# Decoder layer on one core: ScalarE's order in the first two batches of the attention phase, and where batch 0's cosines are stored

## The chip, the cores and the metric

The kernel runs on one NeuronCore of a Trainium2 chip. The core has a matrix engine (TensorE, PE in the profile; PEld is its loading of stationary tiles), a vector engine (VectorE, DVE), an activation engine (ScalarE, ACT), a general engine (GpSimd, POOL) and a queue for synchronisation and DMA (SyncE, SP). Each works through its own instruction list in order, and they wait for each other through semaphores only. The metric is the device time of the program in microseconds (us), lower is better.

## The reference

A decoder layer on 16 batches of 128 x 1024 f32, in three blocks, each followed by an addition of its input and a layer norm:

```python
# 1: causal attention, 16 heads of 64, rotary q and k, w_q, w_k, w_v, w_out 1024 x 1024
scores = where(causal, einsum('bhqd,bhkd->bhqk', q, k), -1e9) / 8
out = einsum('bhqk,bhkd->bhqd', softmax(scores), v) @ w_out.T
# 2: a 3-tap convolution whose taps are weighted by cosines between neighbours of ctx
sim = stack([cos(e, left(e)), cos(e, e), cos(e, right(e))])     # per batch and position
out = einsum('bit,oi->bot', unfolded_x * repeat(sim, C), weight)
# 3: gated MLP with ternary weights: scale = mean|w|, round(w/scale) clipped to -1..1
out = bitlinear(silu(bitlinear(x, w_gate)) * bitlinear(x, w_up), w_down)    # 1024 -> 2752 -> 1024
```

The mean of |w| over each of the three MLP weights is needed before they can be rounded, so these weights are read twice.

## The kernel before

It is written by hand, engine by engine, with semaphores; nothing reorders it. Phase 1 has a prologue and 16 turns, one per batch b. In the prologue the four attention weights are loaded, batch 0's q, k and v are computed from the raw f32 weights (`first_qkv`), and each weight is scaled by its norm and split into a high and a low f16 part. ScalarE writes the high part of tile n (`high_w(n)`, L847), VectorE the low part (`split_w`, L1226); `high_w(n)` waits until the split of tile n-2 is done. Tiles 16 to 23 are w_v, 24 to 31 w_out, and the last of these splits happen in turn 0. The norms come from `square(n)` on ScalarE (L1005) and a small product on TensorE, `w_total(m)` (L573), which VectorE reads in `w_factors(m)`.

A turn b on TensorE: transposes of q and k (`qk_T`, L516), the six half products that make batch b+1's q, k and v (`proj(0..5)`, each 24 products of 128 x 512, L525), the scores of two groups of eight heads (`scores(0)`, `scores(1)`, L627), the transposes of the probabilities (`prob_T(0)`, `prob_T(1)`, L516), probabilities times v (`pv(0)`, `pv(1)`, L649), and the output product of the batch (`out_proj`). In turn 0 batch 1's halves 0 and 2 are already there, and batch 0's output product is computed in turn 1. A product half waits for its PSUM bank to be read: `proj(1)` for `v_chunk(0,1)` on ScalarE, `proj(3)` for the rotary step on VectorE (L1064, L1070). `proj(4)` in turn 0 also waits for the last split of w_v.

VectorE masks the scores and takes their maxima (`mask_max`, L1253 to L1258), ScalarE takes the exponentials with their sums (`exps`, L885, eight instructions per group of eight heads), VectorE normalises (L1266, L1267), TensorE transposes. Each transpose pair and each q/k pair fills two PSUM banks, which ScalarE copies out (`copy_bank`, L817), and `scores` and `pv` wait for these copies.

Beside this, ScalarE sums |w| of the MLP weights in turns 0 to 5: eight chunks of 128 x 1376 a turn (`abs_chunk`, L862), through two buffers (`wch`). SP loads a chunk (`w_load`, L400) when the one that lay in its buffer has been summed. `abs_chunk(-5)` in turn 1 is chunk 3 of turn 0. SP's list holds, in this order, the loads of the chunks, of the transposed x of batch b+2 (L418), of ctx (L423, and L424 for a shifted row), of the residual (L434), and the stores of the three cosine rows (L476, waits for POOL's cosines) and of the block's result (L393). The order on each engine is the order of calls in the function `turn` of that engine; for batches 0 and 1 it is written out apart (`turn_first`, and `if second`), batches 2 to 5 and 6 to 13 are loops.

Phase 2 (convolution and MLP, one turn per batch) follows after turn 15 and begins when phase 1's products are done.

Of the kernel before, what the change touches and what calls it, by code (L numbers as in the profile page):

```python
# [79 lines left out]
def decoder(nc, x, xT_in, ctx, wqT, wkT, wvT, woT, w_ffn, conv_w, cos, sin, causal, ident, out):  # L80
# [4 lines left out]
    with ExitStack() as stack:  # L85
# [270 lines left out]
        def _(sp):  # L356
# [37 lines left out]

            def turn(b, mode, has_next, has_next2):
# [29 lines left out]
                if second:  # L425
                    w_load(0)
                    w_load(1)
                    store_x1(0, xres)
# [31 lines left out]
                if mode != "plain":  # L460
                    for c in range(2, SUMS if mode == "sum" else CUTS):
                        if mode == "cut":
                            w_store(c - 2)
                        w_load(c)
                    if mode == "cut":
                        w_store(CUTS - 2)
                        w_store(CUTS - 1)
# [4 lines left out]
                sp.wait_ge(sims_ready, b + 1)  # L472
                for j, row in ((0, 1), (1, 2), (1, 0)):
                    off = 1 if row == 0 else 0
                    dst = sim_dram[bass.ds(b, 1), row, off:off + D].rearrange("o (p t) -> p (o t)", t=8)
                    sp.dma_start(dst, cosines[:, j]).then_inc(sims_stored, 16)  # L476
# [33 lines left out]
        def _(pe):  # L510
# [99 lines left out]
            def turn(b, mode, has_next, has_next2):  # L610
# [68 lines left out]
                if isinstance(b, int) and b == 0:  # L679
                    qk_T(0)  # L680
                    proj(1)
                    scores(0)
                    qk_T(1)
                    proj(3)
                    scores(1)
                    prob_T(0)
                    proj(4)
                    pv(0)
                    proj(5, 0)
                    prob_T(1)  # L690
                    proj(5, 1)
                    pv(1)
                    pe.wait_ge(roped, 6)
                    transposes(tr_pair(1, 0), [s[:, t * P:(t + 1) * P] for s in (q, k) for t in range(4)])
                    return
# [50 lines left out]
            w_total(3)  # L746
# [66 lines left out]
        def _(act):  # L813
# [42 lines left out]
            def turn(b, mode, has_next, has_next2):  # L856
# [45 lines left out]
                def turn_first():  # L902
                    for w in range(2):
                        copy_bank(w, tr_pair(0, 0), qkT[:, w])
                    for n in range(2 * KT + 4, 3 * KT + 1):
                        high_w(n)
                    act.wait_ge(scores_full, 1)
                    for w in range(2):
                        copy_bank(w, tr_pair(0, 1), qkT[:, w])
                    abs_chunk(0)  # L910
                    exps(0)
                    high_w(3 * KT + 1)
                    for w in range(2):
                        copy_bank(w, tr_pair(0, 2), probT[:, w])
                    exps(1)
                    high_w(3 * KT + 2)
                    oT_high_part(0)
                    abs_chunk(1)
                    act.wait_ge(pv_full, 1)
# [3 lines left out]
                    high_w(3 * KT + 3)  # L923
                    v_chunk(1, 0)
                    v_chunk(1, 1)
                    oT_high_part(1)
                    high_w(3 * KT + 4)
# [7 lines left out]

                if first:
                    turn_first()
                    return
                second = isinstance(b, int) and b == 1
                if not second:  # L940
                    for w in range(2):
                        copy_bank(w, tr_pair(b, 0), qkT[:, w])
# [3 lines left out]
                if second:  # L946
                    abs_chunk(-5)
                exps(0)
                if second:
                    abs_chunk(-4)  # L950
                    abs_chunk(-3)
                elif has_next:
                    ctx_square()
                if not second:
                    abs_chunk(0)
# [5 lines left out]
                if second:  # L961
                    abs_chunk(-2)
                    abs_chunk(-1)
                    ctx_square()
                    abs_chunk(0)
# [54 lines left out]
            square(3 * KT + 7)  # L1020
# [727 lines left out]
```

## Time and profile before

| | |
|---|---|
| time, median of 3 runs | 1411.73 us (1410.52 to 1412.89) |
| the profiled execution | 1411.03 us, of which the span from first to last instruction is 1409.2 us |
| PE busy | 1365.5 us (97%) |
| DVE busy | 1063.0 us (75%) |
| ACT busy | 623.2 us (44%) |
| POOL busy | 214.1 us (15%) |
| mean granted TensorE clock | 0.992 of full |

A row of the timeline gives the start and the duration of a run of like instructions in us, the engine, the source line, output and input tiles, the shapes, the count, and in brackets the idle time of the engine before it and what ended it. f32 products show two records each. Turn 0 begins on TensorE after w_v's products at 62.8 us, turn 1 with a product at 104.80, turn 2 at 172.96.

### The profile page before, as it was taken

The page shows a single profiled execution, that of the slowest core. Times are in us where ns is not written, and L with a number is a line of the kernel's source. Part 1 is how long each engine was busy: PE and PEld are TensorE (multiplying, and loading weights), DVE is VectorE, ACT ScalarE, POOL GpSimd, SP SyncE. Part 2 cuts the span into 40 slices and gives each one's busy share as a digit, 9 for nine tenths or more (in the row PEclk, how much of TensorE's full clock was granted, in tenths as well). Part 3 has the DMA queues.
Part 4 walks back from the last instruction along what each step waited for, and adds up shares of the span by engine and source line. Part 5 has one row for each costly group of instructions (what it writes and reads, how often), then busy time and mean ns, then how long its engine had stood idle before and what let it go on. Part 6 is the DMA issues. An engine that isn't in the chain of part 4 may idle for free.

```text
span 1409.2 us, 23219 instructions
## 1 busy us (share of the span) xinstructions
PE 1365.5 (97%) x7562; PEld 691.9 (49%) x7562; DVE 1063.0 (75%) x1859; ACT 623.2 (44%) x1208; POOL 214.1 (15%) x257
## 2 busy tenths in 40 slices
PE   8989899999999999999999999999999999999997
PEld 3445455555545545554554554444444444444443
DVE  6978355456488677777868778888888888888884
ACT  6867454474455455545535452232222223222321
POOL 0002212213131221221322212000000000000000
PEclk9989999999999999999999999999999999999999
DMA  9514454454434435454453584222222222222200
GB/s 379 220 41 149 154 199 146 138 184 148 169 113 158 162 113 174 141 164 141 140 185 107 133 276 133 76 74 74 74 74 74 74 74 74 74 74 74 74 20 25
DMA packets 63878, 178.96 MB, mean 127 GB/s; under 512 B 15408, under 2 KB 26848, under 8 KB 63840
## 3 DMA queue, kind: packets, MB, share of 16 engines
q1 hardware_dynamic: 63840, 178.48, 38.8%
q8 instruction: 20, 0.33, 0.1%
q14 instruction: 18, 0.15, 0.0%
HBM read 153.02 MB, written 25.43 MB: 127 GB/s over the span
## 4 chain that ended last, share of the span: by engine, by line
issue 42%; PE 42%; POOL 4%; DVE 4%; DMA 4%; ACT 2%; SPq 1%; POOLq 0%; ACTq 0%; DVEq 0%
PE ps L525 32%; PE ps L516 3%; DMA ctx<-ctx 3%; PE ps L595 3%; PE ps L649 2%; PE ps L627 2%; POOL q L1635 1%; DVE weights L1226 1%; ACT prob L885 1%; POOL simw L1688 1%; POOL rstd L1630 1%; ACT weights L847 1%; POOL k L1617 1%; DMA wch<-w_ffn 0%; DMA x_scratch<-weights 0%
## 5 line engine op out<-in xcount | busy, mean ns | idle before, releaser
L525 PE MATMUL ps<-weights,xT 128*128 128x512 f16 x2112 | 473.5, 381 | 0.9 <-ACT v L833 0.9
L525 PEld LDWEIGHTS ps<-weights,xT 128*128 128x128 f16 x2112 | 204.8, 98 | 238.0 <-issue 8.9
L759 PE MATMUL ps<-weights 128*128 128x512 fp8e4 (+1 forms) x1536 | 300.0, 357 | 0.9 <-DMA weights<-ternary_scratch 0.9
L759 PEld LDWEIGHTS ps<-weights 128*128 128x128 bf16 x1536 | 146.9, 98 | 155.8 <-issue 1.3
L525 PE MATMUL ps<-weights 128*128 128x512 f16 x768 | 168.9, 379 | 1.5 <-DVE weights L1272 1.5
L780 PE MATMUL ps<-weights 128*128 128x512 fp8e4 x704 | 158.4, 381 | 0.0
L1030 ACT ACTIVATE weights<-ps,xscale 128x512 f32<-128x512 f32 x96 | 61.8, 644 | 171.7 <-PE ps L759 171.7
L885 ACT ACTIVATE prob<-prob,negmax,undo 128x128 f32<-128x128 f32 x256 | 122.8, 484 | 9.1 <-DVE negmax L1258 9.1
L525 PEld LDWEIGHTS ps<-weights 128*128 128x128 f16 x768 | 75.1, 98 | 90.9 <-DVE weights L1272 1.7
L780 PEld LDWEIGHTS ps<-weights 128*128 128x128 bf16 x704 | 68.0, 98 | 76.8 <-issue 1.8
L1630 POOL TENSOR_TENSOR rstd<-rstd,expo 128x1 f32<-128x1 f32 x32 | 17.9, 559 | 523.8 <-DVE rstd L1152 491.0
L817 ACT COPY qkT<-ps 128x512 f32<-128x512 f32 x64 | 34.3, 588 | 139.3 <-PE ps L516 139.3
L854 ACT CAST weights<-weights 128x1024 f16<-128x1024 f32 x48 | 50.2, 1047 | 69.0 <-DVE weights L1179 64.0
L862 ACT ACTIVATE wch<-wch 128x1376 f32<-128x1376 f32 x48 | 64.6, 1346 | 27.5 <-DMA wch<-w_ffn 27.5
L837 ACT ACTIVATE xT<-weights,magic,xscale 128x1024 f32<-128x1024 f32 x16 | 19.9, 1242 | 127.6 <-DVE xscale L1203 127.6
L1543 DVE SCALAR_TENSOR_TENSOR weights<-ps,xscale,weights 128x512 f32<-128x512 f32 x96 | 65.9, 687 | 7.2 <-PE ps L759 6.8
L1244 DVE SCALAR_TENSOR_TENSOR tern<-wch,thr,below 128x1376 fp8e4<-128x1376 f32 x24 | 55.4, 2308 | 17.8 <-ACT below L877 14.6
L1617 POOL TENSOR_TENSOR k<-rope_c,rope_s 128x512 f32<-128x512 f32 x28 | 41.0, 1463 | 183.1 <-issue 95.5
L1064 DVE SCALAR_TENSOR_TENSOR rope_c<-ps,cosb 128x512 f32<-128x512 f32 x58 | 39.8, 686 | 34.6 <-PE ps L525 29.5
L555 PE MATMUL ps<-weights 128*128 128x512 f16 x288 | 64.8, 379 | 0.0
L1617 POOL TENSOR_TENSOR q<-rope_c,rope_s 128x512 f32<-128x512 f32 x28 | 36.7, 1311 | 162.9 <-DVE rope_s L1070 162.8
L1536 DVE TENSOR_REDUCE hmax<-weights 128x1 f32<-128x512 f32 x96 | 59.9, 624 | 1.2
(171 smaller groups left out, 1813.0 us busy)
## 6 DMA issues: line engine op xcount, KB each, us to landing
wch<-w_ffn SPq DMA_DIRECT2D x96, 688.0 KB, 4.3
wch<-sim_scratch SPq DMA_DIRECT2D x96, 128.0 KB
ternary_scratch<-tern SPq DMA_DIRECT2D x48, 172.0 KB, 1.9
ctx<-ctx SPq DMA_DIRECT2D x16, 512.0 KB
wo_raw<-x_scratch SPq DMA_DIRECT2D x16, 512.0 KB, 3.3
x_in<-xT_in SPq DMA_DIRECT2D x15, 512.0 KB, 6.7
weights<-x SPq DMA_DIRECT2D x15, 512.0 KB, 10.4
x_scratch<-weights SPq DMA_DIRECT2D x15, 512.0 KB, 2.9
```

The lines of the kernel that those rows point to most:

```text
L525: ins = nc.tensor.matmul(ps[:, bank], partsT[:, a, t], weights[:, t, w, half * HALF:(half + 1) * HALF], start=(t == 0 and a + w == 0), sto ...
L555: ins = nc.tensor.matmul(ps[:, c], convw_parts[:, w, kk], conv_parts[:, kk, a, c * HALF:(c + 1) * HALF], start=(kk == 0 and a + w == 0), s ...
L759: ins = nc.tensor.matmul(ps[:, 2 * w + a, 0:n], xqT[:, t], w8m[:, t, at:at + n], start=(t == 0), stop=(t == KT - 1))
L780: return nc.tensor.matmul(ps[:, AC + c], hT[:, t], down8[:, t, c * HALF:(c + 1) * HALF], start=(t == 0), stop=(t == IT - 1))
L854: nc.scalar.copy(conv_parts[:, kk, 0], convG[:, kk + 1]).then_inc(conv_high, 1)
L862: nc.scalar.activation(wch[:, c % 2], wch[:, c % 2], ACT.Abs, accum_out=abs_part[:, bass.ds(b * SUMS + c, 1)]).then_inc(wch_free[c % 2], 1)
L885: ins = nc.scalar.activation(prob[:, r, t], prob[:, r, t], ACT.Exp, scale=undo[:, 0, 0:1], bias=negmax[:, r, t:t + 1], accum_out=rowsum[:, ...
L1030: nc.scalar.activation(silu[:, w, 0:n], ps[:, 2 * w, 0:n], ACT.Silu, scale=xscale[:, 1:2]) \
L1244: nc.vector.scalar_tensor_tensor(out=tern[:, c % 2], in0=wch[:, c % 2], scalar=thr[:, 0:1], in1=below[c % 2], op0=ALU.is_gt, op1=ALU.min, ...
L1536: return st.done(nc.vector.tensor_reduce(hmax[:, c:c + 1], hbuf[:, at:at + n], AX_X, ALU.max, apply_absolute_value=True))
L1543: nc.vector.scalar_tensor_tensor(out=hbuf[:, at:at + n], in0=ps[:, 2 * w + 1, 0:n], scalar=xscale[:, 2:3], in1=silu[:, w, 0:n], op0=ALU.mu ...
L1617: nc.gpsimd.tensor_tensor((q, k)[j % 2][:, j // 2 * HALF:(j // 2 + 1) * HALF], rope_c[:], rope_s[:], ALU.add) \
```

## The change

On ScalarE: (a) the square of tile 31 moves from before batch 0's v copies to behind turn 0's first q/k copies. (b) In turn 0, `high_w(24)` moves from before the second q/k copies to behind the first exponentials, the sum of chunk 0 from before these exponentials to behind `high_w(24)`, `high_w(25)` from before the first probability copies to behind them, `high_w(26)` to behind the first output part and the sum of chunk 1, and `high_w(27)` to behind the v copies and the second output part. (c) Turn 1 has a function of its own, `turn_second`: sum -2 stays ahead of the second exponentials and sum -1 behind them, ahead of the ctx square; the last probability copies stand ahead of sums 2 and 3; sums 4 and 5 stand behind the first v copy instead of ahead of the output part. On TensorE (d) `w_total(3)` moves from the end of the prologue into the middle of `proj(1)`. On SP (e) batch 0's cosines are stored in turn 1, behind chunk loads 0 and 1 (turn 0 ends without them), and chunk loads 2 and 3 of turn 1 stand ahead of the store of batch 0's result.

ScalarE in turn 0, from w_out's last square on, before. `tern,wsq<-wo_raw` is the square of tile 31, `weights<-weights,wnorm` a high part, `qkT` and `probT` the copies out of PSUM, `prob,rowsum` the exponentials, `wch,abs_part` a sum of |w|:

```order
L1005 ACTIVATE tern,wsq<-wo_raw 128x1024
L829 ACTIVATE v<-ps,scale 128x512 x2
L817 COPY qkT<-ps 128x512 x2
L847 ACTIVATE weights<-weights,wnorm 128x1024 x5
L817 COPY qkT<-ps 128x512 x2
L862 ACTIVATE wch,abs_part<-wch 128x1376
L885 ACTIVATE prob,rowsum<-prob,negmax,undo 128x128 x8
L847 ACTIVATE weights<-weights,wnorm 128x1024
L817 COPY probT<-ps 128x512 x2
L885 ACTIVATE prob,rowsum<-prob,negmax,undo 128x128 x8
```

The same place now:

```order
L838 ACTIVATE v<-ps,scale 128x512 x2
L826 COPY qkT<-ps 128x512 x2
L1038 ACTIVATE tern,wsq<-wo_raw 128x1024
L856 ACTIVATE weights<-weights,wnorm 128x1024 x4
L826 COPY qkT<-ps 128x512 x2
L894 ACTIVATE prob,rowsum<-prob,negmax,undo 128x128 x8
L856 ACTIVATE weights<-weights,wnorm 128x1024
L871 ACTIVATE wch,abs_part<-wch 128x1376
L826 COPY probT<-ps 128x512 x2
L856 ACTIVATE weights<-weights,wnorm 128x1024
L894 ACTIVATE prob,rowsum<-prob,negmax,undo 128x128 x8
```

The first exponentials now follow the second q/k copies directly; a high part and a sum stood between.

ScalarE in turn 1, from the first probability copies on, before (`sq<-ctx` is the ctx square, `weights<-ps` a high part of the attention output):

```order
L817 COPY probT<-ps 128x512 x2
L885 ACTIVATE prob,rowsum<-prob,negmax,undo 128x128 x8
L862 ACTIVATE wch,abs_part<-wch 128x1376 x2
L900 ACTIVATE sq<-ctx 128x1152
L862 ACTIVATE wch,abs_part<-wch 128x1376 x2
L893 CAST weights<-ps 128x512
L862 ACTIVATE wch,abs_part<-wch 128x1376 x2
L817 COPY probT<-ps 128x512 x2
L862 ACTIVATE wch,abs_part<-wch 128x1376 x2
```

And now:

```order
L826 COPY probT<-ps 128x512 x2
L871 ACTIVATE wch,abs_part<-wch 128x1376
L894 ACTIVATE prob,rowsum<-prob,negmax,undo 128x128 x8
L871 ACTIVATE wch,abs_part<-wch 128x1376
L909 ACTIVATE sq<-ctx 128x1152
L871 ACTIVATE wch,abs_part<-wch 128x1376
L902 CAST weights<-ps 128x512
L871 ACTIVATE wch,abs_part<-wch 128x1376
L826 COPY probT<-ps 128x512 x2
L871 ACTIVATE wch,abs_part<-wch 128x1376 x2
```

Three sums stand between the second exponentials and the second probability copies where six stood: one of the six is now ahead of the exponentials, two are behind the copies.

SP from turn 0's last six chunk loads to turn 1's result store, before:

```order
L400 DMA wch<-w_ffn 128x1376 x6
L476 DMA sim_scratch<-cosines 128x8 x3
L418 DMA x_in<-xT_in 128x1024
L423 DMA ctx<-ctx 128x1024
L424 DMA ctx<-ctx 127x128
L400 DMA wch<-w_ffn 128x1376 x2
L393 DMA x_scratch<-weights 128x1024
```

And now:

```order
L408 DMA wch<-w_ffn 128x1376 x6
L426 DMA x_in<-xT_in 128x1024
L431 DMA ctx<-ctx 128x1024
L432 DMA ctx<-ctx 127x128
L408 DMA wch<-w_ffn 128x1376 x2
L401 DMA sim_scratch<-cosines 128x8 x3
L408 DMA wch<-w_ffn 128x1376 x2
L393 DMA x_scratch<-weights 128x1024
```

The x and ctx loads no longer stand behind the store of the cosines.

```diff
@@ SP @@
                 if second:
                     w_load(0)
                     w_load(1)
+                    store_sims(0)
+                    w_load(2)
+                    w_load(3)
                     store_x1(0, xres)
...
-                    for c in range(2, SUMS if mode == "sum" else CUTS):
+                    for c in range(4 if second else 2, SUMS if mode == "sum" else CUTS):
...
-                sp.wait_ge(sims_ready, b + 1)
-                for j, row in ((0, 1), (1, 2), (1, 0)):
...
+                if not (isinstance(b, int) and b == 0):
+                    store_sims(b)
@@ TensorE, turn 0 @@
                     qk_T(0)
-                    proj(1)
+                    proj(1, 0)
+                    w_total(3)
+                    proj(1, 1)
                     scores(0)
...
             for m in range(3):
                 first_qkv(m)
-            w_total(3)
@@ ScalarE, turn_first @@
                     for w in range(2):
                         copy_bank(w, tr_pair(0, 0), qkT[:, w])
-                    for n in range(2 * KT + 4, 3 * KT + 1):
+                    square(4 * KT - 1)
+                    for n in range(2 * KT + 4, 3 * KT):
                         high_w(n)
                     act.wait_ge(scores_full, 1)
                     for w in range(2):
                         copy_bank(w, tr_pair(0, 1), qkT[:, w])
+                    exps(0)
+                    high_w(3 * KT)
                     abs_chunk(0)
-                    exps(0)
-                    high_w(3 * KT + 1)
                     for w in range(2):
                         copy_bank(w, tr_pair(0, 2), probT[:, w])
+                    high_w(3 * KT + 1)
                     exps(1)
-                    high_w(3 * KT + 2)
                     oT_high_part(0)
                     abs_chunk(1)
+                    high_w(3 * KT + 2)
...
@@ ScalarE, turn 1 @@
+                def turn_second():
+                    act.wait_ge(scores_full, 3)
+                    for w in range(2):
+                        copy_bank(w, tr_pair(1, 1), qkT[:, w])
+                    abs_chunk(-5)
+                    exps(0)
+                    abs_chunk(-4)
+                    abs_chunk(-3)
+                    act.wait_ge(pv_full, 2)
+                    for w in range(2):
+                        copy_bank(w, tr_pair(1, 2), probT[:, w])
+                    abs_chunk(-2)
+                    exps(1)
+                    abs_chunk(-1)
+                    ctx_square()
+                    abs_chunk(0)
+                    oT_high_part(0)
+                    abs_chunk(1)
+                    act.wait_ge(pv_full, 3)
+                    for w in range(2):
+                        copy_bank(w, tr_pair(1, 3), probT[:, w])
+                    abs_chunk(2)
+                    abs_chunk(3)
+                    oT_high_part(1)
+                    v_chunk(2, 0)
+                    abs_chunk(4)
+                    abs_chunk(5)
+                    v_chunk(2, 1)
+                    high_x(3)
+                    abs_chunk(6)
+                    abs_chunk(7)
@@ ScalarE, prologue @@
             high_w(2 * KT + 3)
-            square(3 * KT + 7)
             v_chunk(0, 0)
```

## Rows read from the trace of the kernel before

**Rows 1.** Part 2 of the page: busy tenths of PE in 40 slices of the span.
```profile
PE   8989899999999999999999999999999999999997
```
**Rows 2.** Timeline of PE, turn 0 and the first product of turn 1.
```profile
64.38 0.39 PE L573 MATMUL ps<-wsq,tern 128*128 128x8 f32 x2 [1.57 <-ACT tern L1005]
...
70.90 1.16 PE L627 MATMUL ps<-qkT 64*128 64x128 f32 x16
...
72.94 5.34 PE L525 MATMUL ps<-weights,xT 128*128 128x512 f16 x24
80.20 1.84 PE L627 MATMUL ps<-qkT 64*128 64x128 f32 x16 [1.92 <-ACT qkT L817]
86.24 1.97 PE L516 MATMUL ps<-idf,prob 128*128 128x128 f32 x8 [4.20 <-DVE prob L1267]
88.01 6.70 PE L525 MATMUL ps<-weights,xT 128*128 128x512 f16 x24
...
104.80 5.34 PE L525 MATMUL ps<-weights,xT 128*128 128x512 f16 x24 [0.86 <-ACT v L833]
```
**Rows 3.** Timeline of PE, turn 1 to the start of turn 3.
```profile
123.64 1.09 PE L516 MATMUL ps<-idf,prob 128*128 128x128 f32 x8
...
153.98 1.98 PE L649 MATMUL ps<-probT,v 128*64 128x128 f32 x16 [6.53 <-ACT probT L817]
155.89 6.87 PE L525 MATMUL ps<-weights,xT 128*128 128x512 f16 x24
...
172.96 0.60 PE L516 MATMUL ps<-idf,q 128*128 128x128 f32 x4
...
223.29 0.60 PE L516 MATMUL ps<-idf,q 128*128 128x128 f32 x4
```
**Rows 4.** Stretches: us, busy (x instructions) of PE, PEld, DVE, ACT, POOL; clock; DMA.
```profile
76.60:114.03 37.43, 30.45 (x185) 17.28 (x184) 27.30 (x51) 28.21 (x59) 0.00 (x0) 0.86 0.12 39
80.50:90.70 10.20, 6.00 (x31) 4.00 (x28) 5.21 (x10) 7.53 (x24) 0.00 (x0) 0.50 0.22 71
152.10:159.00 6.90, 5.02 (x24) 2.79 (x25) 0.00 (x0) 3.52 (x7) 0.38 (x1) 0.51 0.79 236
```
**Rows 5.** Timeline of ACT, turn 0, around the second q/k copies.
```profile
77.99 1.15 ACT L847 ACTIVATE weights<-weights,wnorm 128x1024 f16<-128x1024 f32 x1 [5.20 <-DVE weights L1226]
...
79.99 1.36 ACT L862 ACTIVATE wch<-wch 128x1376 f32<-128x1376 f32 x1
...
81.33 0.49 ACT L885 ACTIVATE prob<-prob,negmax,undo 128x128 f32<-128x128 f32 x1
```
**Rows 6.** Timeline of DVE, turn 0 and the start of turn 1.
```profile
72.05 0.75 DVE L1070 SCALAR_TENSOR_TENSOR rope_s<-ps,sinb 128x256 f32<-128x256 f32 x2
...
76.46 0.23 DVE L1258 TENSOR_SCALAR negmax<-negmax,undo 128x4 f32<-128x4 f32 x1
...
85.28 0.18 DVE L1266 RECIPROCAL rinv<-rowsum 128x4 f32<-128x4 f32 x1 [1.00 <-ACT prob L885]
...
86.11 1.28 DVE L1226 SCALAR_TENSOR_TENSOR weights<-weights,wnorm 128x1024 f16<-128x1024 f32 x1
...
114.03 0.69 DVE L1064 SCALAR_TENSOR_TENSOR rope_c<-ps,cosb 128x512 f32<-128x512 f32 x1
...
121.18 2.21 DVE L1267 TENSOR_TENSOR prob<-prob,rinv 128x512 f32<-128x512 f32 x1
```
**Rows 7.** Timeline of ACT, turn 1, up to the second probability copies.
```profile
140.20 1.16 ACT L900 ACTIVATE sq<-ctx 128x1152 f32<-128x1152 f32 x1 [4.79 <-DMA ctx<-ctx]
...
149.78 1.35 ACT L862 ACTIVATE wch<-wch 128x1376 f32<-128x1376 f32 x1 [4.40 <-DMA wch<-w_ffn]
...
152.83 1.05 ACT L817 COPY probT<-ps 128x512 f32<-128x512 f32 x2
```
**Rows 8.** Timeline of SP's queue, the end of turn 0's list and the ctx load.
```profile
129.44 1.29 SPq L476 DMA_DIRECT2D sim_scratch<-cosines  x3
...
131.30 0.38 SPq L423 DMA_DIRECT2D ctx<-ctx  x1
```

More of the change, by code:

```diff
@@ L393, in store_x1, with store_sims @@
                 sp.dma_start(x1_dram[bass.ds(n, 1)].rearrange("o s d -> s (o d)"), src).then_inc(x1_stored, 16)
+            def store_sims(n):
+                sp.wait_ge(sims_ready, n + 1)
+                for j, row in ((0, 1), (1, 2), (1, 0)):
+                    off = 1 if row == 0 else 0
+                    dst = sim_dram[bass.ds(n, 1), row, off:off + D].rearrange("o (p t) -> p (o t)", t=8)
+                    sp.dma_start(dst, cosines[:, j]).then_inc(sims_stored, 16)
             def turn(b, mode, has_next, has_next2):
@@ L471, in turn @@
                     store_x1(b - 1, xres)
-                sp.wait_ge(sims_ready, b + 1)
-                for j, row in ((0, 1), (1, 2), (1, 0)):
-                    off = 1 if row == 0 else 0
-                    dst = sim_dram[bass.ds(b, 1), row, off:off + D].rearrange("o (p t) -> p (o t)", t=8)
-                    sp.dma_start(dst, cosines[:, j]).then_inc(sims_stored, 16)
+                if not (isinstance(b, int) and b == 0):
+                    store_sims(b)
                 if not has_next:
@@ L922, in turn_first @@
                     high_x(2)
-                    high_w(3 * KT + 3)
                     v_chunk(1, 0)
@@ L926, in turn_first @@
                     oT_high_part(1)
+                    high_w(3 * KT + 3)
                     high_w(3 * KT + 4)
@@ L938, in turn @@
                     return
[L939 to L942, printed above, removed]
+                if isinstance(b, int) and b == 1:
+                    turn_second()
+                    return
+                for w in range(2):
+                    copy_bank(w, tr_pair(b, 0), qkT[:, w])
                 act.wait_ge(scores_full, b * 2 + 1)
@@ L945, in turn @@
                     copy_bank(w, tr_pair(b, 1), qkT[:, w])
-                if second:
-                    abs_chunk(-5)
                 exps(0)
[L949 to L952, printed above, removed]
+                if has_next:
                     ctx_square()
-                if not second:
-                    abs_chunk(0)
+                abs_chunk(0)
                 sign_chunk(0)
@@ L960, in turn @@
                 exps(1)
[L961 to L965, printed above, removed]
                 abs_chunk(1)
```

## The prediction

> **What bounds the kernel now.** I read the busy slices first: TensorE is at nine tenths or more from the sixth slice of 35 us almost to the end [rows 1]. Turn 2 takes 223.29 - 172.96 = 50.33 us [rows 3], and that is TensorE's own work, so from 172.96 us on an edit elsewhere can gain nothing, and an engine that is late by less than its slack costs nothing. What is to be had lies before 172.96. Second I read TensorE's timeline there, for the brackets: idle 1.57 us before `w_total(3)`, 1.92 before the second scores, 4.20 before the first probability transposes, 0.86 before turn 1's first product [rows 2], and 6.53 before `pv(1)` of turn 1 [rows 3]. That is 15.08 us. Third I read the granted clock: it is 0.50 in 80.5 to 90.7 and 0.51 in 152.1 to 159.0 [rows 4]. The first stretch begins right behind the 1.92 us gap, the second inside the 6.53 us one. TensorE was busy for 6.00 and 5.02 us in them; at full rate it would have needed half, so the low clock costs 3.0 and 2.5 us. The rows agree: the product at 88.01 lasts 6.70 and not 5.34 us, the scores at 80.20 1.84 and not 1.16 [rows 2]. In all about 20.5 us can be won at the most.
>
> **The change, part by part.**
>
> *The square and `w_total(3)`.* They leave the 1.57 us gap, but the gap isn't won. `proj(3)` needs the PSUM bank that VectorE's rotary step reads until 72.05 + 0.75 = 72.8 [rows 6], and VectorE's list up to there is unchanged; it starts at 72.94 now [rows 2] and would start at about 72.9 again. TensorE waits some 1.1 us at that point instead of 1.57 earlier. Value: 0. In its new place `w_total(3)` needs a square that now runs behind four copies, an estimated 2 us later than the 64.38 of before [rows 2], and TensorE gets there after half a product, at about 67.0; if this cover of 0.6 fails, VectorE's factors come late by the same, and it has no slack. I take 0, with 0 to 0.5 as the bounds.
>
> *The second q/k copies.* ScalarE holds them back behind a high part that waits until 77.99 for VectorE [rows 5]. Their input, the transposes behind the scores of 70.90, is done by 72.9 at the latest, so they now run at about 72.7 and the scores start when `proj(3)` ends, 72.94 + 5.34 = 78.3, less the overlap of 0.1 with the next. Value: the 1.92 us of idle.
>
> *The exponentials.* They start at 81.33 now, behind a sum that began at 79.99 [rows 5]. Both maxima are there at 76.46 + 0.23 = 76.7 [rows 6], the first 1.6 earlier, at 75.1. So they run from 75.15; the second four, due at 77.1, don't wait. From their start to VectorE's last reciprocal it is 85.28 - 81.33 = 3.95 us [rows 5, 6], which gives 79.1. From there to the transposes it is 86.24 - 85.28 = 0.96, so they start at 80.1, 6.1 us earlier. The scores end at 79.4, and 0.7 us of idle stay.
>
> *The v product behind them.* It needs the last w_v split as well, which VectorE runs after normalising: 86.11 - 85.28 + 1.28 = 2.1 us behind the reciprocal [rows 6], at 81.2. So it starts at 81.3 where it was 88.01 [rows 2]: 6.7 us earlier, and at full clock it lasts 5.34 and not 6.70, so it ends 8.1 us earlier.
>
> *The rest of turn 0.* TensorE's next pieces have 8.1 us of lead and VectorE must give as much. From 76.60 to 114.03 VectorE is busy for 27.30 of 37.43 us [rows 4]; 10.1 us are idle. The exponentials' waits go, and so does the wait for a transpose that ran at half clock. What stays is the 0.14 or so per small semaphore wait, some 0.8 us for ScalarE's high part of x, and 0.3 in w_out's splits: about 2.0. VectorE reaches turn 1 at 114.03 - 8.1 = 105.9. The sums of chunks 0 and 1, and w_out's high parts, fill holes of ScalarE, which is busy for 28.21 of the 37.43. Turn 1's first product starts at about 96.4 (0.75 of the 0.86 idle is found again, as a wait for the low part of x). From that product to turn 1's probability transposes TensorE has 123.64 - 104.80 = 18.8 us of work [rows 2, 3]: 115.2. VectorE gets from its turn start to the second normalised half in 121.18 + 2.21 - 114.03 = 9.4 us [rows 6]: 115.3. The two meet, so VectorE is the next bound there, and any microsecond that it loses TensorE loses. Value of turn 0: 123.64 - 115.35 = 8.3 us (bounds 6.5 and 9).
>
> *Turn 1.* `pv(1)` waits for copies that start at 152.83, behind sums whose chunks come late (4.40 us before the one of 149.78) and behind the ctx square, which waited 4.79 for its load until 140.20 [rows 7]. The ctx load was issued at 131.30, behind the cosine store, which held SP until 129.44 [rows 8]. Now SP gets to it after chunk load 7. That load goes out when sum -3 is done, at about 123.6 before and 115.3 now, so ctx is issued at 116.2 and, with the same 140.20 - 131.30 = 8.9 us, is there at 125.1. ScalarE behind it: exponentials 120.5 to 124.5, sum -1 to 125.9, ctx square to 127.0, sum 0, whose chunk is issued at 119.7 and lands after 7.7 us at the slowest that a chunk took in this stretch, to 128.9, the output part to 129.4, sum 1 to 131.5 (its chunk issued at 126.0, with 4 us; at 7.7 us: 135.2). The transposes to be copied end at about 134.0, so the copies are done at 135.0, with the slow load at 136.2. TensorE comes to `pv(1)` at 155.89 - 1.98 - 6.53 - 8.3 = 139.1. The cover is 4 us, or 3. All of the wait goes: 6.53 us, and with it the clock loss of 2.5. Value: 9.0 us (bounds 4 and 9.2).
>
> *The tail of turn 1.* ScalarE must give batch 3's high x, and VectorE the low one, before turn 2's first product at 172.96 + 0.87 - 17.3 = 156.5. Sums 4 and 5 now stand ahead of it. Their chunks are issued behind the store and reload of the residual, at about 138, and land at 142 and 144; the sums end at 145.5, high x at 147.2 and the low part at 148.5. 8 us of cover: 0. The cosine store in its new place waits for POOL's cosines, which come 8.3 us earlier too, at 121.1, before SP gets there at 126: 0. Turn 2 finds the same list at the same distances, 0.
>
> *Sum.* 8.3 + 9.0 = 17.3 us, taken down to 17.1 because two engines meet at the end of turn 0. 1411.03 - 17.1 = 1393.9 us for the execution profiled (its span would be 1392.1). The median of the runs is 0.7 above this execution, so between them 1394.2.
>
> **The clock, by row and by rule.** In the rows the clock fell behind a gap of 1.92 us and not behind one of 1.57 or 0.86 [rows 2, 4]. What I leave in turn 0 is 1.1, then 0.7 and 0.3 with a transpose between them, all below 1.57, so the clock should hold.
>
> The Trainium skill ("TensorE: Matmul & The Clock Gate", Part 1) says that half rate is the default, that activity releases it, and that the gate runs freely beside the program, so that one kernel meets it in another phase each run. By that rule two gaps of 0.7 and 0.3 near the 1.1 could still fall badly in some executions; the traces show one execution each and can't exclude it. It is the first rival below.
>
> **Rivals.**
>
> *The clock falls once all the same in turn 0.* For: 2.1 us of idle stay between 71.8 and 81.3. Against: they are in three pieces. The price is the 3.0 us of that stretch [rows 4], of which VectorE's own path hides a little: 14.5 us gained, 1396.5.
>
> *VectorE bounds turn 0 and takes back some of it.* It meets TensorE at 115.3. If its waits for ScalarE (high x, w_out's high parts, one of which now stands behind the copies of `prob_T(1)`) stay at 4 us rather than 2, all is late by 2: 15.3 gained, 1395.7.
>
> *Turn 1's wait shrinks but stays.* For: chunk loads share the engines of the DMA with ctx, x and each other, and one took 7.7 us. If sums 0 and 1 each find their chunk 3 us later than I say, the copies end at 141 or 142 and TensorE waits 2 to 3; with a gap like that the clock falls too, 2.5 us: 12 gained, 1399.
>
> *Slower.* The cosine store stands in front of turn 1's chunk loads 2 and 3. SP can't pass it, and behind it stand the residual's store, its reload and the loads of chunks 4 and 5, whose sums are ahead of high x of batch 3. If POOL's cosines came late, turn 2's first product would be late. It decides from 126 us on, the time at which SP gets there, first eats 8 us of cover, and then costs one for one; to lose more than the 17.1 the cosines would have to come after 126 + 8 + 17 = 151, 30 us after the 121.1 worked out above. At 155 it would give 1415. Against it: POOL is empty there.
>
> *Nothing happens*, because the gaps were set by something else: the brackets name ScalarE's instructions for 1.92 and 6.53, and the 4.20 stands behind a late exponential. 1411.
>
> **Chances.** Forecast (16 to 18.5 us gained) 0.68; the clock falls once 0.11; VectorE takes some back 0.09; turn 1's wait stays in part 0.08; slower 0.02; nothing 0.02. The likeliest gives 1394.2, with 1392.5 to 1396 as its own range. Below, the bounds of the parts add up to 18.2, and the bound of all is 20.5, so I go to 1391.8; above, I take in the clock and VectorE and half of the case with turn 1's wait: 1398.8. All of these but the last two are faster. About 0.2% (2.8 us) can be told from no change here. Faster 0.96, same 0.02, slower 0.02.
>
> **What would show it.** In the profile after: no bracket over 1.3 us on TensorE before turn 2; the second scores at 78.2, the first probability transposes at 80.1, the v product at 81.3 and 5.34 long; turn 1's first product near 96.4 and its first probability transposes near 115.3, VectorE's last normalising just ahead of them; `pv(1)` of turn 1 at 139 with no idle; turn 2 at 155.7; the clock at 1.00 from 60 us on; the ctx square of batch 1 near 126. It is wrong if a gap stands before `pv(1)`, if a half-clock stretch remains, or if turn 2's own length is no longer 50.33.

## The result and the profile after

The changed kernel takes 1393.95 us (median of 4 runs, 1391.7 to 1394.55) against 1411.36 us for the kernel before (4 runs, 1410.52 to 1412.89): ratio 0.9869, 95% interval 0.9857 to 0.9880 (the medians by themselves give 0.9877). It is 17.4 us faster; forecast were 17.1 us and 1394.2. The profiled execution took 1394.44 us with a span of 1392.6.

TensorE's timeline, turn 0 and the first product of turn 1 (columns as in [rows 2]):

```profile
64.76 2.75 PE L533 MATMUL ps<-weights,xT 128*128 128x512 f16 x12 [0.91 <-ACT v L838]
...
73.11 5.34 PE L533 MATMUL ps<-weights,xT 128*128 128x512 f16 x24 [0.76 <-DVE rope_s L1102]
78.38 1.16 PE L635 MATMUL ps<-qkT 64*128 64x128 f32 x16
80.23 1.09 PE L524 MATMUL ps<-idf,prob 128*128 128x128 f32 x8 [0.69 <-DVE prob L1299]
81.47 5.34 PE L533 MATMUL ps<-weights,xT 128*128 128x512 f16 x24
...
96.62 5.35 PE L533 MATMUL ps<-weights,xT 128*128 128x512 f16 x24 [0.57 <-DVE xT L1152]
```

The brackets of 1.92 and 4.20 us [rows 2] are gone and 0.69 is left; the 1.57 before `w_total(3)` has become 0.91 and 0.76. The product behind the probability transposes is 5.34 us long again, not 6.70. Turn 1's first product starts at 96.62 where it was 104.80.

The same in turn 1, up to the start of turn 3:

```profile
115.54 1.09 PE L524 MATMUL ps<-idf,prob 128*128 128x128 f32 x8
...
139.28 1.10 PE L657 MATMUL ps<-probT,v 128*64 128x128 f32 x16
140.31 5.35 PE L533 MATMUL ps<-weights,xT 128*128 128x512 f16 x24
...
155.86 0.60 PE L524 MATMUL ps<-idf,q 128*128 128x128 f32 x4
...
206.14 0.60 PE L524 MATMUL ps<-idf,q 128*128 128x128 f32 x4
```

The product after `pv(1)`, 6.87 us long before [rows 3], takes 5.35. `pv(1)` has no bracket where 6.53 us stood [rows 3]. Turn 2 starts at 155.86 instead of 172.96, 17.10 us earlier, and is 50.28 us long as before. ScalarE, turn 1, the rows that answer to [rows 7]:

```profile
126.71 1.17 ACT L909 ACTIVATE sq<-ctx 128x1152 f32<-128x1152 f32 x1 [0.54 <-DMA ctx<-ctx]
...
133.83 1.07 ACT L826 COPY probT<-ps 128x512 f32<-128x512 f32 x2 [2.02 <-PE ps L524]
```

The ctx square no longer waits 4.79 us, and ScalarE now waits for TensorE before the probability copies, not the other way round. What ends last at turn 1's first probability transposes is VectorE's normalising, which is done at 115.48 where the transposes start at 115.54:

```profile
113.27 2.21 DVE L1299 TENSOR_TENSOR prob<-prob,rinv 128x512 f32<-128x512 f32 x1
```

Two stretches of the kernel after: all of turns 0 and 1, and one much later (columns as in [rows 4]):

```profile
60.00:155.86 95.86, 92.78 (x537) 47.81 (x537) 75.36 (x132) 72.58 (x144) 17.61 (x21) 1.00 0.38 126
821.50:824.90 3.40, 2.92 (x7) 1.03 (x8) 2.02 (x6) 1.30 (x2) 0.00 (x0) 0.50 1.04 385
```

Both half-clock stretches of [rows 4] are gone, but a new one of 3.4 us stands in turn 15, in code that the change doesn't touch. (One more, in the last 20 us, is in both traces, behind a gap of 3.78 us that both have.) The rows at that place, of the kernel before:

```profile
834.66 1.09 PE L516 MATMUL ps<-idf,prob 128*128 128x128 f32 x8 [0.54 <-DVE prob L1267]
836.68 1.09 PE L649 MATMUL ps<-probT,v 128*64 128x128 f32 x16 [0.93 <-DVE weights L1272]
839.25 5.35 PE L525 MATMUL ps<-weights 128*128 128x512 f16 x24 [1.47 <-DVE weights L1272]
```

and of the kernel after:

```profile
817.39 1.09 PE L524 MATMUL ps<-idf,prob 128*128 128x128 f32 x8 [0.54 <-DVE prob L1299]
819.42 1.09 PE L657 MATMUL ps<-probT,v 128*64 128x128 f32 x16 [0.93 <-DVE weights L1304]
821.98 6.79 PE L533 MATMUL ps<-weights 128*128 128x512 f16 x24 [1.47 <-DVE weights L1304]
```

The gaps are the same to the hundredth; in one execution the clock holds and in the other it falls and costs 6.79 - 5.35 = 1.44 us. That is why the spans differ by 16.6 and not 17.1 us (0.9 us were won elsewhere in the rest). Differences of 1 to 2 us between single executions can be of this kind. So the experiments below are read by their medians and, where that is finer, by the time from `proj(3)` of turn 0 to turn 2 on TensorE: 100.02 us before, 82.75 after.

### The profile page after: what moved, and what is told of

Read it like the earlier page. It is cut to its first block, busy times and chain, and to the rows that moved or that the text cites. A ratio compares the mean times of both kernels' runs of the same rounds, so it can differ in the third digit from the quotient of the medians.

```text
span 1392.6 us, 23220 instructions
## 1 busy us (share of the span) xinstructions
PE 1362.0 (98%) x7562; PEld 689.2 (49%) x7562; DVE 1063.5 (76%) x1859; ACT 622.4 (45%) x1208; POOL 215.7 (15%) x257
## 4 chain that ended last, share of the span: by engine, by line
PE 51%; issue 40%; POOL 3%; DVE 2%; DMA 2%; ACT 1%; SPq 0%; POOLq 0%; ACTq 0%; DVEq 0%
PE ps L533 40%; PE ps L524 4%; PE ps L603 3%; PE ps L657 2%; PE ps L635 2%; DMA ctx<-ctx 1%; POOL q L1667 1%; POOL rstd L1662 1%; ACT prob L894 1%; DVE weights L1258 1%; POOL simw L1720 0%; PE ps L563 0%; ACT weights L856 0%; DMA weights<-wqT 0%; POOL k L1649 0%
## 5 line engine op out<-in xcount | busy, mean ns | idle before, releaser
L826 ACT COPY qkT<-ps 128x512 f32<-128x512 f32 x64 | 34.3, 588 | 133.8 <-PE ps L524 133.8
```

## The experiments

Each ran beside the kernel before (medians of it 1412.08, 1412.53 and 1412.89 us in the three groups), 4 runs each unless said. Differences "over the changed kernel" are against 1393.95, which was measured beside a median of 1411.36. The kernel before drifts by 1.5 us between these groups, so a difference of less than that is not settled by medians, and the TensorE time decides.

**Turn 0 alone.** The kernel before with the change's lines of turn 0:

```diff
-            w_total(3)            # end of TensorE's prologue
+                    proj(1, 0); w_total(3); proj(1, 1)
-  turn_first of the kernel before
+  turn_first of the change, square(31) in it
```

> The kernel before with turn 0's part of the change alone (square, w_total(3), ScalarE's order in turn 0). My theory: the two gaps of 1.92 and 4.20 us and the first half-clock stretch go, and turn 1 keeps its 6.53 us wait before pv(1) and the low clock behind it. Turn 1's first product at 96.6 us, turn 2 at 172.96 - 8.2 = 164.8, time 8.2 us under the kernel before. Rival (the order in turn 0 only matters together with the earlier loads, as turn 1's chunks and ctx come when they come): turn 1's wait grows by what turn 0 wins, and the time moves by less than 3 us.

Measured: 1404.57 us (1403.27 to 1406.19), 7.5 under the kernel before, ratio 0.9946 (0.9930 to 0.9963). From `proj(3)` to turn 2 it takes 91.84 us, 8.2 less than before. TensorE at `pv(1)` of turn 1:

```profile
146.29 1.98 PE L649 MATMUL ps<-probT,v 128*64 128x128 f32 x16 [6.55 <-ACT probT L818]
```

The wait of 6.53 stands there unchanged as 6.55, with the half clock behind it. What turn 0 wins is kept whole, and the rival, a longer wait in turn 1, is out.

**Turn 1 alone.** The change with turn 0 put back:

```diff
-  turn_first of the change; proj(1, 0); w_total(3); proj(1, 1)
+  turn_first of the kernel before; proj(1), w_total(3) in the prologue
```

> The change with turn 0 (ScalarE, w_total(3)) put back as in the kernel before; turn 1's ScalarE order and SP's list are the new ones. My theory: the parts add up, so this wins what turn 0 alone does not: no wait before pv(1) of turn 1, no half clock there, the gaps of 1.92 and 4.20 us and the half clock in turn 0 remain; 8.9 us under the kernel before. Rival (the parts overlap): under 5 us.

Measured: 1403.60 us (1402.49 to 1405.81), 8.5 under the kernel before, ratio 0.9938 (0.9922 to 0.9955). `pv(1)` has no gap. From `proj(3)` to turn 2: 90.99, 9.0 less. 8.2 + 9.0 = 17.2 of 17.27: the two parts add up.

**The square and `w_total(3)` put back.**

```diff
+            square(3 * KT + 7)     # again ahead of v_chunk(0, 0)
-                    square(4 * KT - 1)
-                    proj(1, 0); w_total(3); proj(1, 1)
+                    proj(1)        # w_total(3) again in the prologue
```

> The changed kernel with the last square and w_total(3) back where they were (the square ahead of batch 0's v copies, w_total(3) at the end of the prologue). The prediction gave this part 0: a gap of 1.4 to 1.6 us before w_total(3), none before the first half product, and proj(3) starting where it does now, for VectorE. Time within 0.3 us of the changed kernel, unless the gap brings the clock down (1.7 us for a short stretch). Rival: the 1.57 us were real and come back, 0.7 to 1.5 us.

Measured: 1393.98 us (1392.81 to 1394.9), ratio 0.9864 (0.9846 to 0.9881), that is 0.0 over the changed kernel. The gap is back, and `proj(3)` starts within 0.2 us of the 73.11 of the changed kernel; from there to turn 2 it is 82.77 against 82.75:

```profile
64.72 0.39 PE L581 MATMUL ps<-wsq,tern 128*128 128x8 f32 x2 [1.54 <-ACT tern L1036]
...
73.28 5.34 PE L533 MATMUL ps<-weights,xT 128*128 128x512 f16 x24
```

A gap of 1.5 us on the busiest engine is worth nothing here, since VectorE's rotary step sets the start of `proj(3)`.

**One high part ahead of the second q/k copies.**

```diff
-                    for n in range(2 * KT + 4, 3 * KT):
+                    for n in range(2 * KT + 4, 3 * KT + 1):
...
                     exps(0)
-                    high_w(3 * KT)
                     abs_chunk(0)
```

> The change with one high part (tile 24) back ahead of turn 0's second q/k copies; the exponentials still stand ahead of the sum. Theory A (the high part, which waits for a split on VectorE until 78 us, is what costs in turn 0): the second scores start at 80.2, the exponentials at about 80.1, the probability transposes at 85.0 after a gap of 3.7 us, the clock falls, and the time is 4.8 us of idle and 2 to 3 us of low clock over the changed kernel: 7.5. Theory B (the sum ahead of the exponentials costs as much as the high part): 2 us of idle over the changed kernel, 2 to 4 in all.

Measured: 1400.81 us (1399.97 to 1401.58), 6.9 over the changed kernel, ratio 0.9920 (0.9902 to 0.9938); `proj(3)` to turn 2 is 6.5 us longer. ScalarE, and TensorE behind it:

```profile
78.53 1.15 ACT L856 ACTIVATE weights<-weights,wnorm 128x1024 f16<-128x1024 f32 x1 [5.20 <-DVE weights L1257]
79.59 1.05 ACT L826 COPY qkT<-ps 128x512 f32<-128x512 f32 x2
```
```profile
80.74 1.16 PE L635 MATMUL ps<-qkT 64*128 64x128 f32 x16 [1.92 <-ACT qkT L826]
85.45 1.97 PE L524 MATMUL ps<-idf,prob 128*128 128x128 f32 x8 [3.55 <-DVE prob L1298]
```

One instruction of 1.1 us that waits 5.20 for VectorE brings back 1.92 + 3.55 - 0.69 = 4.8 us of idle and the half clock, as theory A said. From `proj(3)` to the probability transposes it is 13.30 us before [rows 2], 11.97 here and 7.12 in the changed kernel: 4.85 us hang on the high part, and the other 1.33, the length of a sum, on the sum that stood behind it in the kernel before.

**The sum ahead of the first exponentials.**

```diff
+                    abs_chunk(0)
                     exps(0)
                     high_w(3 * KT)
-                    abs_chunk(0)
```

> The change with the sum of chunk 0 back ahead of turn 0's first exponentials, behind the early q/k copies. Theory A: ScalarE is idle there for 1.39 us anyway, waiting for VectorE's maxima, so the sum of 1.33 us fills the hole and the exponentials start at 75.3 as now: 0, within 0.3 us of the changed kernel. Theory B: the exponentials come 1.3 us later and everything behind them too: 1.3 us over the changed kernel, and a gap of 2 us before the probability transposes with the low clock that follows one.

Measured: 1394.83 us (1394.15 to 1395.25), ratio 0.9875 (0.9857 to 0.9893), 0.9 over the changed kernel by the medians, where 0.3 at the most was expected; but `proj(3)` to turn 2 is 82.76 against 82.75, so nothing of it is from the edit's place. ScalarE:

```profile
73.97 1.36 ACT L871 ACTIVATE wch<-wch 128x1376 f32<-128x1376 f32 x1
...
75.48 0.49 ACT L894 ACTIVATE prob<-prob,negmax,undo 128x128 f32<-128x128 f32 x1
```

The sum fits in the hole before the maxima. Of the change's edits in turn 0 the place of the sum is worth nothing once the copies are early. Behind late copies it was worth the 1.33 us of the run above.

**SP's list as before, ScalarE's order new.**

```diff
-                    store_sims(0)
-                    w_load(2)
-                    w_load(3)
                     store_x1(0, xres)
...
-                    for c in range(4 if second else 2, SUMS if mode == "sum" else CUTS):
+                    for c in range(2, SUMS if mode == "sum" else CUTS):
...
-                if not (isinstance(b, int) and b == 0):
-                    store_sims(b)
+                store_sims(b)
```

> The change with SP's list as before (cosines stored at the end of turn 0, ahead of the x and ctx loads; chunk loads 2 and 3 of turn 1 behind the result's store). The theory of the prediction: the cosine store holds the ctx load back, so the ctx square and with it the probability copies come later; SP gets to it at 121.3, ctx is issued at about 123 instead of 116.6 and lands about 132, the square ends at 133, sums 0 and 1 at about 137 to 139, the copies at 140: 1 to 2 us of wait before pv(1), and the time 1 to 2 us (or 4, with the clock) over the changed kernel. Rival: the order on ScalarE is all of it, the copies are in time even so, and the time is that of the changed kernel within 0.5 us.

Measured: 1397.04 us (1395.32 to 1398.74), 3.1 over the changed kernel, ratio 0.9889 (0.9873 to 0.9906). ScalarE and TensorE in turn 1:

```profile
132.82 1.17 ACT L905 ACTIVATE sq<-ctx 128x1152 f32<-128x1152 f32 x1 [6.17 <-DMA ctx<-ctx]
...
137.60 1.06 ACT L822 COPY probT<-ps 128x512 f32<-128x512 f32 x2
```
```profile
148.35 10.52 PE L529 MATMUL ps<-weights 128*128 128x512 f16 x48 [2.22 <-DVE weights L1300]
```

The ctx square comes 6.1 us later, as I had it (132.8, 133 expected), but the copies are done at 138.7, in time for `pv(1)`, which has no gap. The time is lost one step later: the output product waits 2.22 us for the second part of the attention output, which ScalarE holds behind sums 2 and 3. `proj(3)` to turn 2 is 85.15 us, 2.4 longer. Expected were 1 to 2 us with the clock at full, as it is here, so the size was somewhat too small and the place wrong.

**The cosine store alone put back.**

```diff
-                    store_sims(0)
                     w_load(2)
                     w_load(3)
...
-                if not (isinstance(b, int) and b == 0):
-                    store_sims(b)
+                store_sims(b)
```

> The changed kernel with batch 0's cosine store back at the end of turn 0's list, ahead of the x and ctx loads; chunk loads 2 and 3 of turn 1 stay ahead of the result's store. In the run with SP's whole list as before, the copies for pv(1) were in time (137.6), and TensorE waited 2.2 us before the output product, for the second part of the attention output, which ScalarE had behind sums 2 and 3. Theory L (the loads behind the store and its reload were the cause): 0 to 0.3 us over the changed kernel, no gap before the output product, the ctx square at about 132.5. Theory C (the cosine store was): a gap of 1.5 us or more, 2 to 3 us over the changed kernel.

Measured: 1399.44 us (1398.88 to 1400.47), 5.5 over the changed kernel, ratio 0.9907 (0.9890 to 0.9925). TensorE:

```profile
147.27 5.34 PE L531 MATMUL ps<-weights 128*128 128x512 f16 x24 [1.06 <-DVE weights L1302]
154.67 7.04 PE L531 MATMUL ps<-weights 128*128 128x512 f16 x24 [2.06 <-ACT v L840]
```

and SP's queue:

```profile
122.07 1.29 SPq L401 DMA_DIRECT2D sim_scratch<-cosines  x3
...
123.94 0.38 SPq L431 DMA_DIRECT2D ctx<-ctx  x1
...
124.69 13.52 SPq L408 DMA_DIRECT2D wch<-w_ffn  x4
138.25 0.44 SPq L393 DMA_DIRECT2D x_scratch<-weights  x1
145.73 0.33 SPq L444 DMA_DIRECT2D weights<-x  x1
```

Theory L, that the place of the loads was the cause, is wrong. Theory C names the right edit, the cosine store, but not the way or the size: it said one gap of 1.5 us or more and 2 to 3 us in all. With the cosine store early, ctx late and chunk loads 2 and 3 ahead of the result's store, that store slips to 138.25 (132.22 in the changed kernel) and its reload to 145.73, chunks 4 and 5 with it. Since the change sums 4 and 5 stand ahead of the second v copy, so the second half of the output product waits 2.06 us for its bank, the clock falls behind it, and all is 5.2 us longer from `proj(3)` to turn 2.

**Chunk loads 2 and 3 alone put back.**

```diff
                     store_sims(0)
-                    w_load(2)
-                    w_load(3)
                     store_x1(0, xres)
...
-                    for c in range(4 if second else 2, SUMS if mode == "sum" else CUTS):
+                    for c in range(2, SUMS if mode == "sum" else CUTS):
```

> The changed kernel with chunk loads 2 and 3 of turn 1 back behind the store of batch 0's result and its reload; the cosine store stays in turn 1. Theory L: their chunks land at about 142 and 144 instead of 134.3 and 138.7, sums 2 and 3 end at about 145, the second output part comes at 146 and TensorE waits 1 to 2 us before the output product: 1 to 3 us over the changed kernel. Theory C: no gap, 0. A third outcome, no gap in either, means that each half alone has enough cover and only both together cost.

Measured: 1394.35 us (1391.59 to 1395.79), ratio 0.9862 (0.9844 to 0.9881), `proj(3)` to turn 2 82.76: nothing. With this the four combinations of SP's two edits are complete, all with the new order on ScalarE:

| time, and `proj(3)` to turn 2, us | loads 2 and 3 ahead of the result's store | behind it |
|---|---|---|
| cosine store in turn 1 | 1393.95, 82.75 | 1394.35, 82.76 |
| cosine store in turn 0 | 1399.44, 87.90 | 1397.04, 85.15 |

Moving the cosine store wins 2.7 us (2.4 on TensorE) with the loads behind and 5.5 (5.2) with them ahead. Moving the loads wins nothing beside the moved store and loses 2.4 (2.8) without it.

**SP's new list alone, ScalarE's order old.**

```diff
+                    store_sims(0)
+                    w_load(2)
+                    w_load(3)
                     store_x1(0, xres)
...                                       # and the rest of the change's diff under SP
```

> The kernel before with SP's new list alone. Theory of the prediction: the ctx load comes 5 us earlier or more, the six sums still stand before the probability copies, so the wait before pv(1) shrinks from 6.53 to about 1 us, below what the clock falls behind; but then sums, output part and high x come in the old order and chunks 2 and 3 early: 5 to 8 us under the kernel before. Rival (the number of sums ahead of the copies sets the wait, not SP's list): under 2 us.

Measured (10 runs): 1410.35 us (1407.17 to 1414.69), 1.7 under the kernel before, ratio 0.9990 (0.9977 to 1.0004): not told from no change. TensorE:

```profile
150.94 1.98 PE L657 MATMUL ps<-probT,v 128*64 128x128 f32 x16 [2.45 <-ACT probT L825]
...
160.66 10.52 PE L533 MATMUL ps<-weights 128*128 128x512 f16 x48 [1.94 <-DVE weights L1280]
```

The wait at `pv(1)` shrinks from 6.53 to 2.45 and 1.94 of it turn up before the output product. `proj(3)` to turn 2 is 2.3 us shorter; from turn 1's first product on it is 3.0, and turn 0, which the edit doesn't touch, came out 0.7 longer in this execution. Expected were 5 to 8; the rival's "under 2" is nearer. Neither ScalarE's order nor SP's list does in turn 1 what both do. SP's list is worth about as much on TensorE under the old order of ScalarE, 2.3 to 3.0 us here, as under the new, 2.4 in the run with SP's list as before.

**Four reductions more on VectorE at the end of turn 0.**

```diff
                     split_w(3, range(4, KT))
+                    for i in range(4):      # hmax is not used in phase 1
+                        nc.vector.tensor_reduce(hmax[:, i:i+1], rope_c[:], AX_X, ALU.max)
```

> The changed kernel with four reductions of 0.6 us (128 x 512) more on VectorE behind w_out's last split, at the end of turn 0; their results are not used. The prediction says that VectorE is the next bound there and has no slack against TensorE at turn 1's first probability transposes: all of the 2.4 us come out, a gap of 2.4 before those transposes, and 2.4 us over the changed kernel, 4 with a short stretch of half clock behind the gap. Rival (VectorE has slack there): less than 1.2 us.

Measured: 1397.53 us (1396.73 to 1399.27), 3.6 over the changed kernel, ratio 0.9890 (0.9872 to 0.9907):

```profile
117.92 1.24 PE L524 MATMUL ps<-idf,prob 128*128 128x128 f32 x8 [2.36 <-DVE prob L1299]
```

2.4 us more on VectorE are 2.36 us of wait on TensorE, and 1.7 of low clock behind it: VectorE has no slack there, as forecast. On TensorE it is 4.1 us from `proj(3)` to turn 2, by the medians 3.6; 4 were expected with a stretch of low clock.

**A gap of 2 us and one of 3 before `proj(3)`.** Two and four reductions ahead of the rotary step:

```diff
                     split_w(2, range(4, 6))
+                    # 2 (or 4) times: tensor_reduce(unused, mask of 128 x 512, min)
                     rope(1, 1)
```

> The changed kernel with two reductions of 0.6 us (128 x 512) more on VectorE ahead of the rotary step that proj(3) waits for in turn 0; their results are not used. The gap before proj(3) grows from 0.76 to 2.0 us. Theory A (a gap of 1.9 us brings the clock down, one of 1.57 does not): all is 1.2 us later, and a stretch of half clock begins behind the gap and costs 2 to 3 us: 3 to 4 in all. Theory B (the clock falls only by the sum of idle around it, and the 1.92 us gap of before fell together with the 4.20 one behind it): 1.2 us, and the clock stays at 1.00.

> As the one with two reductions, with four: the gap before proj(3) grows to 3.2 us and all is 2.4 us later. Both theories of the clock expect it to fall here: 2.4 us of delay and 1.7 to 3 us of low clock, 4 to 5.5 in all over the changed kernel. If the clock stays at 1.00 and the time is 2.4 us over, a single gap of 3 us does not bring it down.

Measured: 1395.04 us (1394.47 to 1397.84), ratio 0.9882 (0.9860 to 0.9904), and 1398.52 us (1394.95 to 1399.1), ratio 0.9896 (0.9872 to 0.9921). Timeline of TensorE with two, then with four:

```profile
74.34 7.03 PE L533 MATMUL ps<-weights,xT 128*128 128x512 f16 x24 [1.94 <-DVE rope_s L1102]
```
```profile
75.54 8.08 PE L533 MATMUL ps<-weights,xT 128*128 128x512 f16 x24 [3.13 <-DVE rope_s L1102]
```

And their stretches:

```profile
74.50:77.90 3.40, 3.40 (x9) 1.22 (x8) 3.26 (x7) 1.36 (x6) 0.00 (x0) 0.50 0.00 0
```
```profile
74.30:81.10 6.80, 5.56 (x14) 1.96 (x15) 6.59 (x13) 3.36 (x15) 0.00 (x0) 0.50 0.01 2
```

A single gap of 1.94 us brought the clock to half (1.2 GHz) for 3.4 us and cost 7.03 - 5.34 = 1.7; one of 3.13 for 6.8 us, 2.7. In these two executions it went as theory A said, with a smaller price than the 3.0 of [rows 4]. In both the later 0.69 before the probability transposes vanishes in the delay, so turn 2 comes 2.1 and 4.4 us later (from turn 0's second q transposes on: 86.73 and 88.97 against 84.60).

The medians say less. With two reductions the time is 1.1 us over the changed kernel, where theory A had 3 to 4 and theory B 1.2; with four it is 4.6, inside the 4 to 5.5. And of the four runs with four reductions one took 1394.95 us at a mean clock of 0.998, the other three 1398.05 to 1399.1 at 0.995 to 0.996. That is what an execution would look like in which the clock did not fall behind the 3.13 us gap: 6.8 us at half clock lower the mean by 3.4 / 1396 = 0.0024, an estimate. No trace of it was kept. So it is shown that a single gap of 1.94 us can bring the clock down, not that it does so each time.

## Why the prediction was right, and where not

*What bounds the kernel.* Right: the 17.1 us are all won before turn 2, and turn 2's length is unchanged (50.28 and 50.33).

*The square and `w_total(3)`, 0.* Right, measured 0.0; the gap left was 0.76 at `proj(3)` and 0.91 before the first half product, 1.67 together for the 1.57 that went. The forecast had 1.1 us, all of it at `proj(3)`.

*Copies and exponentials.* Scores 78.38 (78.2 said), probability transposes 80.23 (80.1), v product 81.47 (81.3). Of the 6.2 us between `proj(3)` and these transposes, 4.85 are the high part's and 1.33 the sum's, and the sum's share was there only because the copies were late: with the copies early its place is worth 0.

*Turn 0's value 8.3.* Measured 8.1 on TensorE (123.64 - 115.54), 8.2 and 7.5 by the run of turn 0 alone. VectorE as the next bound: shown with the four reductions. In the working, turn 1's first product should be at 104.80 - 8.1 - 0.86 + 0.75 = 96.6, not 96.4; it came at 96.62.

*Turn 1's value 9.0.* Measured 17.10 - 8.10 = 9.0. The step that failed is the role of the cosine store. I had it hold the ctx load and with it `pv(1)`. In ScalarE's old order that is so in part: SP's list alone takes the wait from 6.53 to 2.45 us, but 1.94 come back before the output product. With the new order the copies for `pv(1)` end at 134.9, 4.4 us ahead of it, and a ctx square that comes 6.1 us later leaves no gap there; the delay comes out at the output product. How much each of ScalarE's moves in turn 1 is worth by itself stays open, since they were only measured together. Copies at 133.8 said 134.0; ctx square 126.7 said 125.9.

*The tail of turn 1, 8 us of cover.* The low x part ended at 150.17 + 1.28 = 151.5, not 148.5, since chunk 3 took 6.89 us to land and the result's store 7.78. The cover was 5 us. I also looked only at high x and not at the second v copy that the same two sums now stand before; it ended at 149.0, and the output product's second half needs it at 150.7. 1.7 us of cover was the thinnest place of the change, and the run with the cosine store put back falls there. That this part came out at 0 was luck: the 8 us that the forecast leaned on weren't there.

*The clock.* In the changed kernel it held in turns 0 and 1, as forecast, though not "at 1.00 from 60 us on": in turn 15 it fell and cost 1.44 us. The reason given, that a gap of 1.57 is safe and one of 1.92 is not, is too simple. A gap of 1.94 alone brought it down, but in the run of turn 1 alone one of 1.75 did too, and in turn 15 the same three gaps (0.54, 0.93, 1.47) did in one execution and not in the other. This fits the rule cited ahead from the Trainium skill ("TensorE: Matmul & The Clock Gate", Part 1), that the gate runs freely beside the program. No trace here shows it falling on the gaps left in turn 0, and that doesn't exclude it.

*Slower, nothing.* POOL's cosines were there at 121.50, SP got to them at 126.57, so the store waited for nothing. The gaps of 1.92, 4.20 and 6.53 us went, so they were set by what the brackets name.

## What to carry to other kernels

On an engine that runs in order, look first for the instruction that itself waits for a third engine: it delays all behind it by its wait, where a ready one costs its own length or, in a hole, nothing. Work out what each idle gap is worth by what sets the next start, and when a queue's entries are moved, follow every consumer behind each load, not only the one that waits now. Of two edits of one list, one can lose time alone and cost nothing beside the other, as the chunk loads did here (2.4 us and 0), so they are measured in all four combinations.

## What the runs showed of the hardware

Short idle gaps of TensorE can cost more than their length. In the profiled executions 1.94 us of idle brought 3.4 us at half clock (1.7 us of time) and 3.13 us brought 6.8 (2.7). Ahead of `w_total(3)` a gap of 1.75 us (turn 1 alone) brought 3.4 us at half clock, and gaps of 1.57 (the kernel before) and 1.54 (the square put back) did not. The same gaps of 0.54, 0.93 and 1.47 us in a row brought the clock down in one execution and not in another, 1.44 us apart. A chunk load of 688 KB took 3.9 us to land at its fastest and 9.8 us where it was issued right behind the two ctx loads (124.62 to 134.42, SP's list as before).

The last normalising ahead of turn 1's probability transposes takes 2.21 us (113.27 to 115.48) and not the 0.69 of the same instruction elsewhere. It runs beside a product of 128x1024 on GpSimd (112.05 to 114.94), in the kernel before as in the changed one (121.18, beside 119.95 to 122.84). So some 1.5 us of VectorE's path to that bound are this one instruction; no run moves GpSimd's product away, so that it is the cause is not shown.
